# A selective scan whose skip term and running sum move from VectorE to TensorE, and whose state copies move to ScalarE

## What is computed

```python
def _selective_scan(x, dt, Bm, Cm, A, D):
    dA = jnp.exp(dt[..., None] * A)
    dBx = (dt * x)[..., None] * Bm[:, :, None, :]
    def step(h, inputs):
        dA_t, dBx_t, C_t = inputs
        h = dA_t * h + dBx_t
        y = jnp.einsum('bdn,bn->bd', h, C_t)
        return (h, y)
    ...
    return jnp.swapaxes(ys, 0, 1) + x * D[None, None, :]

def _mamba_dir(h, ...):
    ...
    y = _selective_scan(x, dt, Bm, Cm, A, D)
    y = y * jax.nn.silu(z)
    return y @ out_proj_w.T
```

## Time and profile before

| | us |
|---|---|
| median of 3 runs | 2834.26 |
| lowest and highest | 2833.05, 2835.2 |
| the profiled execution's own time | 2835.8 |
| its span, first to last instruction | 2834.0 |
| preparing block of the Mamba layer in it | about 714 to 803.5 |
| scan block in it | 803.7 to about 1232.3 |

### The profile page before, as it was taken

One profiled execution on the slowest core, in us unless ns is written; L12 is line 12 of the kernel. 1 busy time (PEld: TensorE's weight loads), 2 busy tenths in 40 slices (PEclk: granted clock), 3 DMA queues, 4 the chain that ended last, 5 costly groups with the idle time before them and its releaser, 6 DMA issues. The chain is left out here.

```text
span 2834.0 us, 46661 instructions
## 1 busy us (share of the span) xinstructions
PE 2320.7 (82%) x19181; PEld 968.9 (34%) x19181; DVE 2215.0 (78%) x3086; ACT 1910.5 (67%) x1990; POOL 1074.2 (38%) x421
## 2 busy tenths in 40 slices
PE   4677777788846666786699998999879989999996
PEld 2122222255312222243333342333544533333334
DVE  5788888868899999986699838997640358899984
ACT  4999999932643333335499958998432369999981
POOL 5999999912069998932000400004100000000000
PEclk8999999979878988898899999999989989999998
DMA  2011111110034444401311020002010030110000
GB/s 78 1 45 45 57 53 66 50 56 8 26 130 164 163 161 150 163 9 46 76 21 29 13 43 1 13 13 50 8 42 0 22 84 16 44 34 19 16 9 27
DMA packets 67166, 145.55 MB, mean 51 GB/s; under 512 B 13683, under 2 KB 30431, under 8 KB 66240
## 3 DMA queue, kind: packets, MB, share of 16 engines
q1 hardware_dynamic: 66944, 142.47, 17.2%
HBM read 117.99 MB, written 24.25 MB: 50 GB/s over the span
## 5 line engine op out<-in xcount | busy, mean ns | idle before, releaser
L828 POOL TENSOR_TENSOR l0a_diff_pool<-l0a_A,l0a_a_of_t 128x2048 f32<-128x2048 f32 x128 | 531.7, 4202 | 31.2 <-ACT l0a_a_of_t L843 30.7
L2124 ACT ACTIVATE l2x_pT<-ps 128x1024 f32<-128x1024 f32 x512 | 470.2, 1165 | 13.3 <-PE ps L2082 13.3
L2276 ACT ACTIVATE l3he_pT<-ps 128x1024 f32<-128x1024 f32 x480 | 445.2, 1062 | 18.4 <-PE ps L2210 18.4
L1438 PE MATMUL ps<-l1s_hc,all_ident 128*128 128x512 f32 x512 | 285.1, 710 | 155.2 <-POOL l1s_hc L1409 100.8
L774 DVE SCALAR_TENSOR_TENSOR l0a_diff_dve<-l0a_A,l0a_pos,ps 128x512 f32<-128x512 f32 x512 | 344.7, 740 | 30.3 <-PE ps L619 30.2
L1400 POOL TENSOR_TENSOR l1s_dBx<-l1a_dtx,l1a_Bs 128x1024 f32<-128x1024 f32 x128 | 297.5, 2354 | 111.9 <-POOLq L1134 111.9
L1424 ACT ACTIVATE ps<-l1a_dt,l1a_A 128x1024 f32<-128x1024 f32 x128 | 143.1, 1118 | 268.0 <-DVE l1s_hc L1483 215.7
L2082 PE MATMUL ps<-l2m_Qs,l2m_Ks 75*32 75x512 bf16 x4096 | 274.0, 386 | 13.3 <-DMA l2m_Qs<-l2m_mparts 9.0
L2210 PE MATMUL ps<-l3h_Qs,l3h_Ks 75*32 75x512 bf16 x4096 | 274.9, 384 | 9.9 <-DVE ps L2281 9.9
L2097 PE MATMUL ps<-l2x_pT,l2m_Va 128*9 128x512 f32 x2048 | 270.0, 598 | 8.4 <-DVE l2s_oT L2690 3.0
L860 ACT ACTIVATE l0a_diff_pool<-l0a_diff_pool 128x2048 f32<-128x2048 f32 x128 | 237.3, 1901 | 25.8 <-POOL l0a_diff_pool L828 25.7
(11 more groups left out here) (493 smaller groups left out, 3672.3 us busy)
## 6 DMA issues: line engine op xcount, KB each, us to landing
l1a_Bs<-l1a_bc SPq DMA_DIRECT2D x64, 512.0 KB, 3.6
l1s_Cs<-l1a_bc SPq DMA_DIRECT2D x64, 512.0 KB, 4.6
l0a_band_rows<-l0a_band SPq DMA_DIRECT2D x32, 512.0 KB, 6.6
l0a_band<-l0a_exps SPq DMA_DIRECT2D x14, 512.0 KB
l2m_Ks<-l2m_parts SPq DMA_DIRECT2D x36, 128.0 KB
l2m_Qs<-l2m_parts SPq DMA_DIRECT2D x72, 64.0 KB
l3h_Qs<-l3h_parts SPq DMA_DIRECT2D x72, 64.0 KB
l0a_band<-l0a_zero SPq DMA_DIRECT2D x8, 512.0 KB, 7.4
```

The costliest lines, as they stand in the source:

```text
L828: pool.tensor_tensor(out, window(s), atb[:, p % 2, :].unsqueeze(1).broadcast_to([P, 4, CH]), ALU.subtract).then_inc(diff_pool, 1)
L1438: mm = pe.matmul(g.ps[:, (4 + 2 * h + q) * CH:(5 + 2 * h + q) * CH], g.ident[:, :], hc[:, m % NHC, q * CH:(q + 1) * CH], start=(n == 0), s ...
L2124: act.activation(pT[:, turn % NPT, :], g.ps[:, slot * QC:(slot + 1) * QC], ACT.Exp).then_inc(expd, 1)
L2276: act.activation(pT[:, (4 * m + j) % NPT, :], g.ps[:, slot(turn)], ACT.Exp).then_inc(expd, 1)
```

## The change

It has four parts.

- The skip term of direction 1 leaves DVE (L1299 is gone). POOL, in the preparing block, multiplies the identity by D of direction 1 into the columns of `win` that are no longer needed (two 128x128 products). In the scan block PE adds x_r D_r to y by a matrix product with that diagonal.
- y starts from U: at the first step of groups 0, 1 and 3 PE first adds U to y by a product with the identity (`seed`). Groups 1 and 2, which cover the same half of time, share one sum in PSUM, with no reading between. DVE's `gather` (U + y, then times sz) becomes `gate`, y times sz, run after group 2 and after group 3 only. Between groups 0 and 1 ACT copies y to U.
- The last state is copied by ACT (`last_of`), between the end of step m - 2 and the exponential of step m, with a wait for the copy.
- DVE waits for its own scan in `weigh` only, no more after every scan.

```diff
+                @block.gpsimd
+                def _(pool):
+                    pool.wait_ge(xps, HV)
+                    for h in range(HV):
+                        pool.tensor_tensor(win[:, h * P:(h + 1) * P], g.ident[:, :], Dp[:, 1, h:h + 1].broadcast_to([P, P]), ALU.mult).then_inc(diag, 1)
...
-                        if i == 0:
-                            dve.tensor_scalar(U[:, h, :], xc[:, 0, h, :], Dp[:, 0, h:h + 1], None, ALU.mult).then_inc(skipd, 1)
-                        else:
-                            dve.wait_ge(skipd, h + 1)
-                            dve.scalar_tensor_tensor(U[:, h, :], xc[:, 1, h, :], Dp[:, 1, h:h + 1], U[:, h, :], ALU.mult, ALU.add).then_inc(skipd, 1)
...
+            def last_of(m):
+                gr, i, half, n, h = place(m)
+                to = hs[:, m // EVERY % 2, :] if on_pool(m) else hpair(m)
+                end = 0 if i else TH - 1
+                return state[:, i, n * HV + h:n * HV + h + 1], to[:, end:end + 1]
+
+            def saved_up_to(m):
+                gr, rest = divmod(m, SPG)
+                return (gr + 1) // 2 * SPG + (rest + 1 if gr % 2 == 0 else 0)
...
+                        if m >= 2 and place(m - 2)[0] % 2 == 0:
+                            act.wait_ge(scd, m - 1)
+                            act.copy(*last_of(m - 2)).then_inc(saved, 1)
+                            act.wait_ge(saved, saved_up_to(m - 2))
                         act.activation(hpair(m), dt[:, i, h, half * TH:(half + 1) * TH], ACT.Exp,
                                        scale=Al[:, i, h, n:n + 1]).then_inc(dad, 1)
+                        if m == SPG + 3:
+                            for k in range(HV):
+                                act.wait_ge(accd, SPG - HV + k + 1)
+                                act.copy(U[:, k, 0:TH], g.ps[:, (4 + 2 * k) * CH:(6 + 2 * k) * CH]).then_inc(y_read, 1)
...
+                    def seed(gr, half, h):
+                        for q in range(2):
+                            at = slice(half * TH + q * CH, half * TH + (q + 1) * CH)
+                            y = g.ps[:, (4 + 2 * h + q) * CH:(5 + 2 * h + q) * CH]
+                            if gr != 2:
+                                pe.matmul(y, g.ident[:, :], U[:, h, at], start=True, stop=False)
+                            if gr >= 2:
+                                pe.matmul(y, win[:, h * P:(h + 1) * P], xc[:, 1, h, at], start=False, stop=False)
...
-                        if n == 0 and gr:
-                            pe.wait_ge(y_read, HV * (gr - 1) + h + 1)
+                        if n == 0:
+                            if gr == 1:
+                                pe.wait_ge(y_read, h + 1)
+                            if gr == 3:
+                                pe.wait_ge(gated, h + 1)
+                            seed(gr, half, h)
...
-                        dve.wait_ge(scd, m + 1)
-                        if gr % 2 == 0:
-                            end = 0 if i else TH - 1
-                            dve.tensor_copy(state[:, i, n * HV + h:n * HV + h + 1], to[:, end:end + 1]).then_inc(saved, 1)
 
                     def weigh(m):
                         k = m // HV
+                        dve.wait_ge(scd, m + 1)
...
-                    def gather(gr):
+                    def gate(gr):
                         _, i, half, _, _ = place(gr * SPG)
                         at = slice(half * TH, (half + 1) * TH)
                         for h in range(HV):
-                            y = g.ps[:, (4 + 2 * h) * CH:(6 + 2 * h) * CH]
                             dve.wait_ge(accd, gr * SPG + SPG - HV + h + 1)
-                            step(dve.tensor_tensor(U[:, h, at], U[:, h, at], y, ALU.add))
-                            dve.nop().then_inc(y_read, 1)
-                            if i:
-                                dve.tensor_tensor(U[:, h, at], U[:, h, at], sz[:, h, at], ALU.mult).then_inc(gated, 1)
+                            dve.tensor_tensor(U[:, h, at], sz[:, h, at], g.ps[:, (4 + 2 * h) * CH:(6 + 2 * h) * CH], ALU.mult).then_inc(gated, 1)
...
-                        if m % SPG == HV - 1 and m > SPG:
-                            gather(m // SPG - 1)
-                    gather(NG - 1)
+                        if m == 3 * SPG + HV - 1:
+                            gate(2)
+                    gate(3)
```

More of the change, by code:

```diff
@@ L1321, in _ @@
                         conv(n)
-                    for n in range(2 * HV):
-                        skip(n)
+                    for h in range(HV):
+                        skip(h)
                     one_more(0)
@@ L1352, in mamba @@
             weighed, weighed_pool = r2.sem("weighed"), r2.sem("weighed_by_pool")
[L1353 removed]
+            accd, y_read = r2.sem("accumulated"), r2.sem("y_read")
             gated, yps, xad = r2.sem("gated"), r2.sem("y_in_psum"), r2.sem("x_added")
@@ L1457, in _ @@
                 def _(dve):
-                    step = Steps(dve, s1)
                     def scan(m):
```

12 lines of the change are left out of this document (6 added, 6 removed).

## The result

| | before | after |
|---|---|---|
| median, us | 2833.66 (4 runs, 2832.89 to 2835.2) | 2808.52 (4 runs, 2807.01 to 2811.99) |
| ratio, with its 95% interval | | 0.9913 [0.9898, 0.9928] |
| profiled execution, us | 2835.8 | 2809.22 |
| its span, us | 2834.0 | 2807.0 |

The change makes the kernel 25.1 us faster. I had forecast 2816.9 us, 17.4 gained, in a range of 2812.5 to 2823.5.

What follows compares the result with a forecast made beforehand. DVE was taken to set the pace (busy 417.5 of 428.3 us), POOL close behind. Terms 5.1 + 4.6 + 9.0 - 0.5 - 0.5 - 0.3 = 17.4 us off 2835.8 gave 2818.4, the median 1.5 lower: 2816.9, range 2812.5 to 2823.5.

Steps and rivals of the forecast that it cites:

- state copies leave DVE: Scan block: 64 copies move to ACT, each freeing only 0.08 us of DVE's path; 5.1 us gained.
- DVE's wait for its own scan: Scan block: without it a scan right behind POOL's scan starts 0.11 us earlier, 42 steps; 4.6 us gained.
- gathers: Between groups: those after groups 0 and 1 vanish, two gates replace that after group 2; 9.0 us gained.
- second skip: Preparing block: removing 4.61 us from DVE only lengthens its wait for ACT's logarithm; 0 gained.
- POOL's diagonals: Preparing block: POOL's two 128x128 products may push back DVE's first convolutions; -0.5 us, bounds 0 to -1.0.
- PE's seeds: Starts of groups 1 and 3: added products at PE's low clock level may delay weighings; -0.5 us (0 to -1.5).
- POOL the later one: Groups 0 and 2: POOL, at 9.27 us per three steps, falls behind DVE's 9.14; -0.3 us (0 to -1).
- rival A: Scan block: two scans cannot overlap, the second starts only when the first has ended; gain 13, 2821 us, chance 0.10.
- The three deductions: Losses taken off for POOL's diagonals (-0.5), PE's seeds (-0.5) and POOL falling behind DVE (-0.3 us).
- Rival E: Preparing and scan blocks: the skip counts after all, or POOL and PE cost nothing; 2810 to 2814 us, chance 0.03.
- rival C: Scan block: PE at its low clock level throughout, about 45 us slower, 2880 us; chance 0.02.
- signs for wrong: Scan block: DVE waiting for PE over 1.5 us at four weighings, for every third step's exponential, or for dBx over 1.

Runs made afterwards that it cites:

- the experiment above: Kernel before, with only the state copies moved to ACT and the wait for DVE's own scan moved to the weighing; 2823.98 us, ratio 0.9971.

## Why the prediction was wrong in size and right in kind

| step | predicted gain | measured | from |
|---|---|---|---|
| state copies leave DVE | 5.1 | 5.1 | 0.24 of the 0.38 per three steps in groups 0 and 2 |
| DVE's wait for its own scan | 4.6 | 5.9 | 0.14 per pair of scans, 42 pairs |
| gathers | 9.0 | 9.1 | 2.84, 2.8 and 5.70 - 2.26; also what is left of the 20.1 between first and last scan |
| second skip | 0 | 0 | skip back on DVE: preparing block 87.2 both times |
| POOL's diagonals | -0.5 | 0 | preparing block 87.3 and 87.2 |
| PE's seeds | -0.5 | 0 | weighing 36 at 917.52, sums done at 917.06 |
| POOL the later one | -0.3 | 0 | no wait of DVE for `dBx` |
| behind the last scan of the block | 0 | 0.2 | 17.5 and 17.3; chance, by the other profiles |
| sum | 17.4 | 20.3 | scan block 20.3 |
| the rest of the program | 0 | 4.8 | 25.1 less 20.3 |

**State copies.** Right. Only the 0.08 between starts counted, and ACT had the room, 0.77 us at the closest case. Copy and wait cost ACT 0.19 to 0.22 us, as taken.

**The wait.** The mechanism is right and rival A false: scan to scan is 2.20. The size was off by 0.03 for each pair. I took the pair from "weighing to scan", and so expected an early start only; the second scan also lasts 0.03 less (2.27 for 2.30 in group 0, 2.33 for 2.36 in group 3). 42 x 0.03 = 1.3 us. The rule of the Trainium skill weighed here (VectorE: DVE Perf Modes, section "The DRAIN you can't avoid") would have given 0; the start at 860.26, ahead of 860.34, does not agree with it, but does with the same section's remark that an instruction that isn't held starts earlier, which the prediction left out.

**Gathers.** Right: 2.84 and 2.8 to nothing, and 5.70 to two gates, forecast at 2.3, measured at 2.26 from the first gate to the next scan. After group 3 nothing was gained: what the block has outside its first-to-last-scan stretch is 17.5 us before and 17.3 after.

**Skip.** Right, with its waits: forecast 2.9 + 4.6 = 7.5 us of waiting for ACT, measured 7.20.

**The three deductions.** Together they took 1.3 us off for things that did not happen. The diagonals do collide with the convolutions, but I charged the wrong engine: POOL lost 3.9 us, DVE 0.04. The Trainium skill's rule (SBUF — State Buffer, section "Who interferes with whom") gave -1.0. It also says that the order of issue decides who has to wait, and the rows agree: DVE's convolution had started at 719.30, 0.12 ahead of POOL's product, and POOL was held; in the third gather of the experiment above POOL's spread had started first (1111.27 against 1111.38), and DVE was held. The seeds did run at the lower level at first, but the level rose behind the first five records or so, and 0.46 us were left. POOL fell behind nearly as worked out (9.22 us a round, start to start, against 9.27). The 2.1 us that it may fall behind were nearly used up at the end of group 2, with 0.23 left, but DVE never waited. Each had a bound of 0 that I kept, but set the value inside the interval on the side of loss. Rival E ("POOL and PE cost nothing") had a chance of 0.03, far too low for three deductions of which each rested on a row of another place. Its 2810 to 2814 also don't follow from the sum: with all three at 0 the prediction's own terms give 18.7 gained, 2815.6. (A slip without effect stands in rival C: 552 x 0.85 is 469, not 471.)

**The rest.** The block's 20.3 alone would give 2834.3 - 20.3 = 2814.0, inside the range. What took the result out of it is a term that the sum has at nothing without a reason: the part outside the block was put at no change, with "the spread of runs about 1 on each side", read from three runs of one set. Over all sets single runs of the kernel before lay 13.7 us apart, and the part behind the block 9.5. So the step that failed for the range is this one, 4.8 us where the sum has 0, and its cause stays open. The steps that failed for the forecast are the mis-sized wait (1.3) and the deductions (1.3).

What the prediction named as signs came as it said: periods of 9.1 and 9.3, a scan that starts before the other's end, copies of 0.2 on ACT, a block of about 410. None of its signs for wrong appeared.

## What to carry to other kernels

On the engine that sets the pace count starts, not durations: a copy of 0.15 us cost 0.08, and the periods worked out from the starts of five rows (9.14 and 9.32) held over 128 steps within 0.03 us. A wait of that engine for its own last instruction has a price (0.14 us for a pair of scans here), and so has a second wait for the same one (0.06), while waits that are met as the engine still works cost nothing in these rows. So put one wait where it is needed and none where it is not. After a gain, work out what is left of each margin: here 0.46 us at PE's seeds and 0.23 us at POOL's products, so a still faster DVE may have to wait for either. Before a range is written, look at how far apart executions of the whole program lie, in the layers that the change doesn't touch too; three agreeing runs of one set say little of that.
